# Chosen experts' inner activations turned by 32x32 blocks on VectorE and a trip through DRAM, instead of by TensorE

## The chip, the cores and the metric

The kernel runs on one core of one Trainium2 chip. The metric is the device time of one execution in microseconds (us), from the first to the last instruction of the core. Engine names in the profile: PE is TensorE's matmuls, PEld its weight loads, DVE is VectorE, ACT is ScalarE, POOL is GpSimd, SP is SyncE; a q behind a name (SPq) is that engine's sequencer, which issues DMAs.

## The reference, cut to what matters

Four layers with residuals follow each other. The change lies in the first, a mixture of experts over 64 batches of 64 tokens with 256 channels:

```python
rw = softmax(router_logits); w, sel = top_k(rw, 2)          # two experts of 8 for each batch
def _gemma_mlp(x, gate_w, up_w, down_w):                    # 256 -> 1024 -> 256
    g = einsum('bsh,hi->bsi', x, gate_w)
    u = einsum('bsh,hi->bsi', x, up_w)
    return einsum('bsi,ih->bsh', gelu(g) * u, down_w)       # gelu(g) * u: the inner activations
out = sum over the two chosen experts of w_e * mlp_e(x)  +  mlp_shared(x)
x = x + out            # then layers 1, 2 and 3, which the change does not touch
```

The product with `down_w` contracts over the 1024 inner channels, so for TensorE the inner activations must stand with channels, not tokens, on the partitions.

## The kernel before

Every engine has its own hand-written program; semaphores (`wait_ge`, `then_inc`) are the only order between them. Nothing is moved by a scheduler.

The batches are sorted by chosen expert. A group is 128 tokens: two batches with one expert (60 full groups), or two batches with two experts (four such pairs, each worked as two half groups; the code calls them mixed, `at.half` is 0 or 1). That makes NR0 = 68 group slots in a row, one loop of NMIXED0 = 4 rounds of BODY = 17 slots with two slots ahead of it and two behind. The groups before them belong to the shared expert, as do those after them, which are interleaved with layers 1 and 2. "Chosen stage" below is the stretch of these 68 slots, about 182 to 785 us of the span.

A full group has two halves (h = 0, 1) of 512 inner channels. For each, TensorE computes gate and up (`up_gate`, L713 to L715: three passes of float32r parts, 12 matmuls of 512 columns) with tokens on the partitions. ScalarE takes the gelu (L1242), VectorE multiplies with up into `hid` (L1744). TensorE then turns `hid` by four 128x128 transposes against `ident` into `turn_ps` in PSUM (`turn`, L783). ScalarE copies it as high part `hh` (`hidden_hi`, L1252), VectorE subtracts to get the low part `hl` (`hidden_lo`, L1751: one operand in PSUM, one in SBUF), and TensorE multiplies both with the down weights (`down`, L801 to L804). VectorE weighs and adds the result (`add`, L1815 and L1819), SyncE stores it to `chosen_rows` in DRAM (`store_chosen`, L355). In slot g TensorE's order is: up_gate half 0 of g, turn half 1 of g - 1, down half 0 of g - 1, up_gate half 1 of g, turn half 0 of g, down half 1 of g - 1. So down comes one slot behind up_gate.

VectorE also makes the low part of the next x (`split_x`, L1734: both operands in SBUF). GpSimd loads the float32 weights of the next expert in pieces of 512 KB into `raw` and splits each in two parts (`split`, L559 and L561: two operations on 1024 columns, SBUF to SBUF). It starts an expert's six pieces when the last group of the expert before last has been added, and then waits for the next such moment. There are eight such stretches of splitting in the chosen stage, about 34 us each. SyncE's queue holds, in program order per slot: the x loads for the slot after next (`load_skill`, waits for `xl_done`), in four of 17 slots two or four 512 KB pieces of weights for the mixed pair (`load_mixed0`, L363), and `store_chosen`, which waits for `acc_done`.

Of the kernel before, what the change touches and what calls it, by code (L numbers as in the profile page):

```python
# [31 lines left out]
F32 = mybir.dt.float32  # L32
F32R = mybir.dt.float32r
I32 = mybir.dt.int32
ALU = mybir.AluOpType
# [3 lines left out]
P = 128  # L39
NB, S, D = 64, 64, 256  # L40
E = 8
# [12 lines left out]
TURNLESS = 2 * (EARLY - FIRST)  # L54
# [41 lines left out]
FIRST_TWO = place_at(-1, BODY - 2), place_at(-1, BODY - 1)  # L96
LAST_TWO = place_at(NMIXED0, 0), place_at(NMIXED0, 1)


def build(nc, x, xT, cond, condT, w0, w1, mask, b1, w2, b2, w3, b3, out):  # L100
    mixes = nc.dram_tensor("mixes", (WPIECES, P, NU * P), F32, kind="Internal").ap()
    x3 = nc.dram_tensor("x3", (NB, S, D), F32, kind="Internal").ap()
    chosen_rows = nc.dram_tensor("chosen_rows", (NB, P, D), F32, kind="Internal").ap()

    with ExitStack() as ctx:
# [72 lines left out]
        hm = [acc[:, NSH + 25 + h, :] for h in range(2)]  # L178
# [66 lines left out]
        hh_done, hl_done = sem("hh_done"), sem("hl_done")  # L245
        down_done, acc_done, add_step = sem("down_done"), sem("acc_done"), sem("add_step")
# [33 lines left out]
        def table_values(engine, at, top):  # L280

            return nc.values_load_multi_w_load_instructions(
                at, engines=[engine.engine], min_val=0, max_val=top,
                skip_runtime_bounds_check_because="the routing bounds what the table holds")[1]

# [3 lines left out]
        def _(sp):  # L289
# [56 lines left out]
            def load_skill(g, p, at):  # L346
                slot = 2 * at.full if at.half is None else 2 * FULL0 + 2 * at.mixed
                batches = table_values(sp, source[0:1, bass.ds(slot, 2)], NB - 1)
                sp.wait_ge(xl_done, g - 1)
# [47 lines left out]
            for dst, src in ((b12, b1), (b2s, b2)):  # L397
                sp.dma_start(dst, src.rearrange("(a d) -> a d", a=1).broadcast_to([P, D])).then_inc(biases_in, 16)
            for c in range(DC):
                sp.dma_start(b1c[:, c:c + 1], b1[P * c:P * (c + 1)].rearrange("(p a) -> p a", a=1))\  # L400
                    .then_inc(biases_in, 16)
            for k in range(2):
                load_skill(S0 + 2 + k, k, place_at(0, k))
            for k in range(NSTAGE):
                sp.wait_ge(spilled[k], 16 * WPIECES // NSTAGE)
            with sp.Fori(0, NMIXED0) as m:
                for k in range(BODY):
                    g = S0 + BODY * m + k
                    load_skill(g + 4, k % 2, place_at(m, k + 2))
                    if k < 2:  # L410
                        load_mixed0(m, 0, ((0, 1, 2, 3), (4, 5))[k], S0 + BODY * m)
                    at = place_at(m, k - 2)
                    if at.half != 0:
                        store_chosen(g, k % 2, at)
                    if k in (HALVES[0] + 2, HALVES[0] + 3):
                        load_mixed0(m, 1, ((0, 1, 2, 3), (4, 5))[k - HALVES[0] - 2], S0 + BODY * m + HALVES[0] + 3)
# [12 lines left out]
            load_late(0)  # L429
            load_late(1)  # L430
            store_chosen(S1 - 4, 0, place_at(NMIXED0 - 1, BODY - 2))
            store_chosen(S1 - 3, 1, place_at(NMIXED0 - 1, BODY - 1))
# [255 lines left out]
        def _(pe):  # L688
# [49 lines left out]
            def up_gate_mixed(g, at, h):  # L738
# [3 lines left out]
                for ps, k, done in ((gate_ps[h], 0, gate_done), (up_ps[h], 1, up_done)):  # L742
                    if h == 0:
                        pe.wait_ge(mixed0_in[k], 64 * at.mixed + 32 * at.half + 32)
                    for c in range(DC):
                        part = slice(c * 512 + D * h, c * 512 + D * (h + 1))
                        mm = both_batches(ps, chunk(xm, c), [mixed0_w[2 * k + j][:, part] for j in range(2)], D,
                                          c == 0, c == DC - 1)
# [29 lines left out]
            def turn(h, n2, first=False, chunks=4):  # L778
# [3 lines left out]
                for c in range(chunks):  # L782
# [116 lines left out]
            def chosen_group(g, p, at, before_at):  # L899

                def before_down(h, e):
                    if before_at.half is None:
                        down(g - 1, 1 - p, h, e, 2 * g - 2 + h)
                    else:
                        down_mixed(g - 1, 1 - p, before_at, h)

                e = load_expert(at) if at.half is None else None
                for h in range(2):
# [4 lines left out]
                    if h == 0:  # L913
# [1233 lines left out]
```

## Time and profile before

| | us |
|---|---|
| median of 3 runs | 1191.1 |
| lowest and highest run | 1189.87, 1192.92 |
| span of the profiled execution | 1190.3 |
| median less that span | 0.8 |

The span is the profiled execution's own time: what lies around it is not recorded apart. A row of the profile names a line of the kernel, the engine and the operation, the tile written and the one read, and either one duration or the count, the sum and the mean. Matmuls are pipelined: their rows overlap, and the step from one start to the next is what one costs.

### The profile page before, as it was taken

To read this page: it belongs to the slowest core of one execution; us is meant where nothing else is said; L and a number is where in the kernel's file an instruction comes from. 1 tells how busy PE (TensorE), PEld (TensorE's weight loads), DVE (VectorE), ACT (ScalarE), POOL (GpSimd) and SP (SyncE) were. 2 spreads that over 40 slices of the span, in tenths; PEclk is the share of its full clock that TensorE was granted. 3 is DMA by queue.
4 is the path that set the end of the run, shared out by engine and by line. 5 is a ranking of instruction groups with operands and counts; after the bars stand their busy time and mean duration, and the time that the engine had idled before them with its cause. 6 is when DMAs were issued, how large, how long until landed. Compare 5 with 4: busy or idle time off the path is not lost.

```text
span 1190.3 us, 25584 instructions
## 1 busy us (share of the span) xinstructions
PE 1171.9 (98%) x7406; PEld 1001.3 (84%) x7407; DVE 613.2 (52%) x1119; ACT 435.0 (37%) x845; POOL 462.0 (39%) x296
## 2 busy tenths in 40 slices
PE   8999999999999999999999999999999999899998
PEld 7999998788787888878788787889999999678876
DVE  6775775444444444454544454456555555434443
ACT  4355532222222322222222222222222232566664
POOL 3277688108145045180635481010000000888840
PEclk9999999999999999999999999999999999999999
DMA  7279866243253324352253531046644446578653
GB/s 209 63 252 327 286 203 222 67 134 99 68 172 107 126 64 138 100 184 84 83 157 114 183 88 50 18 140 176 182 134 132 132 131 241 169 223 244 212 151 117
DMA packets 159578, 177.88 MB, mean 149 GB/s; under 512 B 68480, under 2 KB 134272, under 8 KB 157440
## 3 DMA queue, kind: packets, MB, share of 16 engines
q1 hardware_dynamic: 145808, 126.83, 35.1%
q0 software_dynamic: 13680, 49.81, 13.7%
q8 instruction: 61, 1.00, 0.3%
q14 instruction: 29, 0.24, 0.1%
HBM read 143.04 MB, written 33.55 MB: 148 GB/s over the span
## 4 chain that ended last, share of the span: by engine, by line
PE 91%; DMA 3%; DVE 2%; POOL 1%; SPq 1%; issue 1%; ACT 1%; ACTq 0%; POOLq 0%; DVEq 0%
PE bank L713 14%; PE bank L714 14%; PE bank L715 14%; PE bank L802 9%; PE bank L1152 6%; PE bank L783 5%; PE bank L734 4%; PE bank L801 4%; PE bank L1181 3%; PE bank L995 2%; PE bank L853 2%; PE bank L1130 2%; PE bank L855 2%; PE bank L854 2%; PE bank L1161 1%; PE bank L804 1%
## 5 line engine op out<-in xcount | busy, mean ns | idle before, releaser
L559 POOL TENSOR_TENSOR W<-raw,one 128x1024 fp32r<-128x1024 f32 x79 | 150.2, 1901 | 565.7 <-DVE acc L1815 269.5
L1744 DVE TENSOR_TENSOR FS<-bank,FS 128x512 f32<-128x512 f32 (+1 forms) x200 | 133.7, 669 | 320.5 <-PE bank L715 276.3
L1242 ACT ACTIVATE FS<-bank 128x512 f32<-128x512 f32 (+1 forms) x200 | 116.1, 580 | 326.4 <-PE bank L715 299.7
L713 PE MATMUL bank<-W,RS 128*128 (+1 forms) x512 | 202.8, 396 | 1.9 <-DVE W L1856 1.9
L714 PE MATMUL bank<-W,RS 128*128 (+1 forms) x512 | 200.6, 392 | 0.0
L715 PE MATMUL bank<-W,RS 128*128 (+1 forms) x512 | 200.3, 391 | 0.0
L561 POOL TENSOR_TENSOR W<-raw,W 128x1024 fp32r<-128x1024 f32 x79 | 191.8, 2428 | 6.2
L802 PE MATMUL bank<-W,RS 128*128 x480 | 188.6, 416 | 0.0
L1252 ACT ACTIVATE RS<-bank 128x512 fp32r<-128x512 f32 x128 | 76.6, 598 | 152.1 <-PE bank L783 152.1
L713 PE MATMUL bank<-RS,W 128*128 128x256 f32 x448 | 129.1, 288 | 1.0 <-DVE RS L1734 1.0
L715 PE MATMUL bank<-RS,W 128*128 128x256 f32 x448 | 126.6, 283 | 0.0
L714 PE MATMUL bank<-RS,W 128*128 128x256 f32 x448 | 126.6, 283 | 0.0
L713 PEld LDWEIGHTS bank<-W,RS 128*128 128x128 f32 x512 | 96.2, 188 | 25.7 <-issue 6.2
L715 PEld LDWEIGHTS bank<-W,RS 128*128 128x128 f32 x512 | 96.2, 188 | 21.1
L714 PEld LDWEIGHTS bank<-W,RS 128*128 128x128 f32 x512 | 96.2, 188 | 19.3
L1751 DVE TENSOR_TENSOR RS<-bank,RS 128x512 fp32r<-128x512 f32 x128 | 88.4, 691 | 35.7 <-ACT RS L1252 35.7
L801 PE MATMUL bank<-W,RS 128*128 x360 | 101.1, 281 | 0.0
L802 PEld LDWEIGHTS bank<-W,RS 128*128 128x128 f32 x480 | 90.6, 189 | 11.3
L713 PEld LDWEIGHTS bank<-RS,W 128*128 128x128 f32 x448 | 85.6, 191 | 1.3 <-issue 1.2
L783 PEld LDWEIGHTS bank<-ident,FS 128*128 128x128 f32 x544 | 67.2, 141 | 22.6 <-issue 6.2
L714 PEld LDWEIGHTS bank<-RS,W 128*128 128x128 f32 x448 | 85.7, 191 | 0.1
L715 PEld LDWEIGHTS bank<-RS,W 128*128 128x128 f32 x448 | 85.6, 191 | 0.0
(227 smaller groups left out, 2051.7 us busy)
## 6 DMA issues: line engine op xcount, KB each, us to landing
raw<-in_w POOLq DMA_DIRECT2D x87, 512.0 KB, 4.3
acc<-in_w SPq DMA_DIRECT2D x70, 512.0 KB, 4.7
mixes<-acc SPq DMA_DIRECT2D x16, 1024.0 KB, 6.3
W<-mixes SPq DMA_DIRECT2D x16, 1024.0 KB, 6.2
FS<-in_xT SPq DMA_DIRECT2D x200, 64.0 KB, 2.7
chosen_rows<-acc SPq DMA_DIRECT2D x64, 128.0 KB, 1.7
acc<-chosen_rows SPq DMA_DIRECT2D x128, 64.0 KB, 2.1
acc<-in_b SPq DMA_DIRECT2D x8, 640.0 KB, 10.9
```

The source lines that it names most:

```text
L559: pool.tensor_tensor(hi, raw[:, k, :], ones_like(PIECE), ALU.mult).then_inc(done, 1)
L561: pool.tensor_tensor(lo, raw[:, k, :], hi.bitcast(F32), ALU.subtract).then_inc(done, 1)
L713: pe.matmul(ps, ah, bh, start=(i == 0), stop=False)
L714: pe.matmul(ps, ah, bl, start=False, stop=False)
L715: mm = pe.matmul(ps, al, bh, start=False, stop=(i == n - 1))
L783: mm = pe.transpose(chunk(turn_ps[h], c), chunk(hid[h], c), ident[:, :])
L801: pe.matmul(ps, chunk(hl[h], c), w2_[:, 0, :], start=False, stop=False)
L802: mm = pe.matmul(both, chunk(hh[h], c), w2_, start=(h == 0 and c == 0), stop=(h == 1 and c == 3))
L1242: act.activation(gl[h][:, 0:n], gate_ps[h][:, 0:n], ACT.Gelu_apprx_tanh).then_inc(gelu_done, 1)
L1252: act.activation(hh[h], turn_ps[h][:, :], ACT.Copy).then_inc(hh_done, 1)
L1744: TT(hid[h][:, 0:n], up_ps[h][:, 0:n], gl[h][:, 0:n], ALU.mult).then_inc(hid_done, 1)
L1751: TT(hl[h], turn_ps[h][:, :], hh[h].bitcast(F32), ALU.subtract).then_inc(hl_done, 1)
```

## The change

TensorE no longer turns the chosen experts' activations. VectorE transposes each `hid` half in its 32x32 blocks (`hidden_squares`), SBUF to SBUF, into `square[h]`. ScalarE issues a DMA that writes this to a DRAM buffer `squares` (`write_square`, one per half, runs of 512 B), and SyncE issues one DMA per group that reads it back with the blocks in turned places into `hidT` in SBUF (`read_hidT`, 512 KB, runs of 1 KB). The copy to `hh` and the subtraction to `hl` now read `hidT` in SBUF, not PSUM. The down weights' rows are permuted on the host to fit the order in which the channels come out, and a mixed half takes every fourth block of gate and up columns. Down now comes two slots behind up_gate, and so do `add` and `store_chosen`. SyncE's bias loads and second late x load move behind the chosen stage.

The pieces below are in this order: SyncE (`read_hidT`, its loop), TensorE (`chosen_group`), ScalarE, VectorE.

```diff
+            def read_hidT(s, p, at):
+                n = D if at.half is None else P
+                if isinstance(s, int):
+                    sp.wait_ge(hl_done, 2 * (S0 + s))
+                sp.wait_ge(squares_out, 32 * s + 32)
+                sp.dma_start(hidT.rearrange("p (a y) -> p a y", a=4)[:, :, 0:n],
+                             squares[p].rearrange("(a i) (g y) -> (i g) a y", a=4, g=4)[:, :, 0:n])\
+                    .then_inc(hidT_in, 16)
...
+                for k in range(BODY):
+                    s, at = 2 + BODY * m + k, place_at(m, k - 2)
+                    if at.half != 0:
+                        load_skill(S0 + s + 2, k % 2, place_at(m, k + 2))
...
+                    if at.half != 0:
+                        store_chosen(S0 + s - 2, k % 2, at)
+                    else:
+                        load_skill(S0 + s + 2, k % 2, place_at(m, k + 2), added=S0 + s - 1)
+                    read_hidT(s, k % 2, place_at(m, k))
...
-                    if h == 0:
-                        turn(1, 2 * g - 1, chunks=4 if before_at.half is None else 2)
-                        before = load_expert(before_at) if before_at.half is None else None
-                    else:
-                        turn(0, 2 * g, chunks=4 if at.half is None else 2)
-                    before_down(h, before)
+                    if s == 0:
+                        down_shared(g - 2, 2 + h)
+                    elif s > 1:
+                        if h == 0:
+                            before = load_expert_at(s - 2)
+                        down_chosen(s - 2, h, before)
...
+            def write_square(s, p, h, at):
+                n = D if at.half is None else P
+                act.wait_ge(squared, 2 * s + h + 1)
+                act.dma_start(squares[p].rearrange("p (g y) -> p g y", g=4)[:, :, n // 2 * h:n // 2 * (h + 1)],
+                              square[h][:, 0:2 * n].rearrange("p (g x) -> p g x", g=4)).then_inc(squares_out, 16)
+            def hidden_hi_chosen(s, h, at):
+                act.wait_ge(hidT_in, 16 * s + 16)
+                act.wait_ge(down_done, 2 * (S0 + s) + h - 1)
+                if at.half is None:
+                    act.activation(by_chunk(hh[h]), turned_hid(h), ACT.Copy).then_inc(hh_done, 1)
...
+            def hidden_squares(s, h, at):
+                dve.wait_ge(hid_done, 2 * (S0 + s) + h + 1)
+                if not (isinstance(s, int) and s == 0):
+                    dve.wait_ge(squares_out, 32 * s)
+                dve.transpose(square[h][:, 0:n], hid[h][:, 0:n]).then_inc(squared, 1)
+            def hidden_lo_chosen(s, h, at):
+                dve.wait_ge(hh_done, 2 * (S0 + s) + h + 1)
+                if at.half is None:
+                    TT(by_chunk(hl[h]), turned_hid(h), by_chunk(hh[h].bitcast(F32)), ALU.subtract).then_inc(hl_done, 1)
```

The order in each engine's program, for a full group in the loop. On VectorE before, one slot with its two halves: hid is TENSOR_TENSOR FS<-bank,FS, the low part is RS<-bank,RS, the low part of x is RS<-FS,RS, or a COPY ahead of a mixed group.

```order
L1741 REGISTER_ALU [waits up_done,gelu_done]
L1744 TENSOR_TENSOR FS<-bank,FS 128x512 [waits turn_done]
L1751 TENSOR_TENSOR RS<-bank,RS 128x512 [waits hh_done]
L1730 REGISTER_ALU
L1732 COPY acc<-FS 128x128 [waits xh_done]
L1738 REGISTER_ALU
L1741 REGISTER_ALU [waits up_done,gelu_done]
L1744 TENSOR_TENSOR FS<-bank,FS 128x512 [waits turn_done]
L1751 TENSOR_TENSOR RS<-bank,RS 128x512 [waits hh_done]
L1815 ISA [waits acc_done,down_done]
L1815 TENSOR_SCALAR acc<-bank,weight 128x256
```

On VectorE now, the same stretch of a slot (X and acc are `square[0]` and `square[1]`, routing is `hidT`):

```order
L1819 TENSOR_TENSOR FS<-bank,FS 128x512 [waits squared]
L1826 REGISTER_ALU [waits hid_done]
L1827 STREAM_TRANSPOSE X<-FS 128x512 [waits squares_out]
L1788 REGISTER_ALU
L1792 TENSOR_TENSOR RS<-FS,RS 128x256 [waits xh_done]
L1813 REGISTER_ALU
L1819 TENSOR_TENSOR FS<-bank,FS 128x512 [waits squared,up_done,gelu_done]
L1827 STREAM_TRANSPOSE acc<-FS 128x512 [waits squares_out,hid_done]
L1832 TENSOR_TENSOR RS<-routing,RS 128x512 [waits hh_done] x2
L1896 ISA [waits acc_done,down_done]
L1896 TENSOR_SCALAR acc<-bank,weight 128x256
```

Each half has a transpose behind its product, and the two subtractions of the group before now stand together at the slot's end, ahead of the addition.

On ScalarE now, one slot (FS<-bank is the gelu, RS<-FS the high part of x, RS<-routing the copy to `hh` of the group before):

```order
L1276 ACTIVATE FS<-bank 128x512 [waits hid_done]
L1270 ACTIVATE RS<-FS 128x256 [waits up_done,xraw_in1]
L1288 ISA
L1289 DMA squares<-X 512x1x128 [waits squared]
L1273 REGISTER_ALU
L1276 ACTIVATE FS<-bank 128x512 [waits hid_done,gate_done]
L1294 ISA
L1297 ACTIVATE RS<-routing 128x512 [waits down_done,hidT_in]
L1288 REGISTER_ALU
L1289 DMA squares<-acc 512x1x128 [waits squared]
L1297 ACTIVATE RS<-routing 128x512 [waits down_done,hidT_in]
```

Before, each copy stood behind a gelu and waited for `turn_done`; now the two copies wait for the DRAM read, and the second write stands between them.

On SyncE now, one slot (before, the last two rows were not there):

```order
L369 REGISTER_ALU
L314 ISA [waits xl_done]
L314 DMA FS<-in_xT 128x2x64
L314 ISA
L314 DMA FS<-in_xT 128x2x64
L377 ISA [waits acc_done]
L377 DMA chosen_rows<-acc 128x256
L424 ISA
L425 DMA routing<-squares 128x4x256 [waits squares_out]
```

The read stands behind the store, and so behind the store's wait for the addition.

## Rows read from the trace of the kernel before

**Rows 1.** The page's busy times (us, share of the span, instructions).
```profile
PE 1171.9 (98%) x7406; PEld 1001.3 (84%) x7407; DVE 613.2 (52%) x1119; ACT 435.0 (37%) x845; POOL 462.0 (39%) x296
```
**Rows 2.** The chain that ended last, by engine, then by line.
```profile
PE 91%; DMA 3%; DVE 2%; POOL 1%; SPq 1%; issue 1%; ACT 1%; ACTq 0%; POOLq 0%; DVEq 0%
PE bank L713 14%; PE bank L714 14%; PE bank L715 14%; PE bank L802 9%; PE bank L1152 6%; PE bank L783 5%; PE bank L734 4%; PE bank L801 4%; PE bank L1181 3%; PE bank L995 2%; PE bank L853 2%; PE bank L1130 2%; PE bank L855 2%; PE bank L854 2%; PE bank L1161 1%; PE bank L804 1%
```
**Rows 3.** Timeline of TensorE, half a full group (start us, us, what).
```profile
200.39 0.60 PE L783 MATMUL bank<-ident,FS 128*128 128x128 f32 x4
200.74 0.48 PE L802 MATMUL bank<-W,RS 128*128 x1
201.06 0.28 PE L804 MATMUL bank<-W,RS 128*128 x1
...
202.24 0.39 PE L713 MATMUL bank<-W,RS 128*128 x1
...
204.97 0.60 PE L783 MATMUL bank<-ident,FS 128*128 128x128 f32 x4
```
**Rows 4.** Lines L1751 (whole span) and L1734 (225 to 780 us): min/median/max ns.
```profile
L1751 DVE TENSOR_TENSOR RS<-bank,RS x128: 678/691/693, 19.2 to 780.5; 128x512 fp32r<-128x512 f32 x128
...
L1734 DVE TENSOR_TENSOR RS<-FS,RS x56: 412/415/2385, 229.1 to 772.2; 128x256 fp32r<-128x256 f32 x56
```
**Rows 5.** Busy by stretch: PE, PEld, DVE, ACT, POOL, clock, DMA share, GB/s.
```profile
269.00:303.00 34.00, 34.00 (x194) 27.43 (x193) 17.31 (x28) 9.94 (x20) 28.82 (x17) 1.00 0.37 106
303.00:341.00 38.00, 38.00 (x201) 30.87 (x200) 16.05 (x31) 10.47 (x20) 0.60 (x1) 1.00 0.37 111
```
**Rows 6.** DMA issues of the whole span: count, KB each, median us to landing.
```profile
acc<-in_w SPq DMA_DIRECT2D x70, 512.0 KB, 4.7
...
W<-mixes SPq DMA_DIRECT2D x16, 1024.0 KB, 6.2
...
chosen_rows<-acc SPq DMA_DIRECT2D x64, 128.0 KB, 1.7
acc<-chosen_rows SPq DMA_DIRECT2D x128, 64.0 KB, 2.1
...
x<-raw SPq DMA_DIRECT2D x16, 256.0 KB, 2.2
```
**Rows 7.** Timeline behind a group's last down, and of SyncE's queue.
```profile
320.42 0.60 ACT L1252 ACTIVATE RS<-bank 128x512 fp32r<-128x512 f32 x1 [1.21 <-PE bank L783]
321.05 0.69 DVE L1751 TENSOR_TENSOR RS<-bank,RS 128x512 fp32r<-128x512 f32 x1 [0.22 <-ACT RS L1252]
321.93 0.48 DVE L1815 TENSOR_SCALAR acc<-bank,weight 128x256 f32<-128x256 f32 x1 [0.18 <-PE bank L802]
322.54 0.48 DVE L1819 SCALAR_TENSOR_TENSOR acc<-bank,weight,acc 128x256 f32<-128x256 f32 x1
323.19 0.35 SPq L355 DMA_DIRECT2D chosen_rows<-acc  x1
...
329.10 1.94 SPq L363 DMA_DIRECT2D acc<-in_w  x4
```
**Rows 8.** Timeline of GpSimd: first and second piece of an expert, next expert.
```profile
269.76 1.88 POOL L559 TENSOR_TENSOR W<-raw,one 128x1024 fp32r<-128x1024 f32 x1 [55.13 <-DVE acc L1815]
...
275.42 1.91 POOL L559 TENSOR_TENSOR W<-raw,one 128x1024 fp32r<-128x1024 f32 x1
...
341.01 1.88 POOL L559 TENSOR_TENSOR W<-raw,one 128x1024 fp32r<-128x1024 f32 x1 [37.37 <-DVE acc L1815]
```
**Rows 9.** L1734 alone, summed over six stretches in which GpSimd splits (us).
```profile
sum 203.00, DVE 26.58; mean DVE 4.43
```
**Rows 10.** The page's DMA queue of GpSimd: packets, MB, share of 16 engines.
```profile
q0 software_dynamic: 13680, 49.81, 13.7%
```
**Rows 11.** Timeline at the end of the chosen stage: turn of x1 waits.
```profile
791.30 0.65 PE L984 MATMUL bank<-ident,routing 128*128 128x128 f32 x4 [1.47 <-DVE routing L1919]
```

More of the change, by code:

```diff
@@ L53 @@
 NU = NSH // 2
-TURNLESS = 2 * (EARLY - FIRST)
 S0, S1 = EARLY, EARLY + NR0
@@ L177, in build @@
         xm, held, scaled = acc[:, NSH + 24, :], acc[:, NSH + 27, :], acc[:, NSH + 28, :]
-        hm = [acc[:, NSH + 25 + h, :] for h in range(2)]
+        hm = [acc[:, NSH + 31, :], routing[:, 5 * D:6 * D]]
+        square = [X1[:, :], acc[:, NSH + 25:NSH + 27, :].rearrange("p a d -> p (a d)")]
+        hidT = routing[:, 0:I0]
         chosen_out = [acc[:, NSH + 29 + r, :] for r in range(2)]
@@ L781, in turn @@
                     pe.wait_ge(hl_done, n2 - 1)
-                for c in range(chunks):
+                for c in range(4):
                     mm = pe.transpose(chunk(turn_ps[h], c), chunk(hid[h], c), ident[:, :])
@@ L897, in pair_shared, with down_chosen, load_expert_at, chosen_group @@
                     mix(2 * q + 1)
[L899 to L903, printed above, removed]
[L904 to L907 removed]
+            def down_chosen(s, h, e):
+                if place(s).half is None:
+                    down(S0 + s, s % 2, h, e, 2 * (S0 + s) + h)
+                else:
+                    down_mixed(S0 + s, s % 2, place(s), h)
+            def load_expert_at(s):
+                return load_expert(place(s)) if place(s).half is None else None
+            def chosen_group(s):
+                g, p, at, before = S0 + s, s % 2, place(s), None
+                e = load_expert_at(s)
                 for h in range(2):
@@ L1043, in _ @@
             pe.sem_inc(down3_done, 1)
-            last = load_expert(LAST_TWO[1])
             pe.wait_ge(split_step, 12 * SHARED_LATE + 12)
-            up_gate_late(0, 0, 0)
-            turn(1, 2 * S1 - 1)
-            down(S1 - 1, 1, 0, last, 2 * S1 - 2)
-            up_gate_late(0, 0, 1)
-            down(S1 - 1, 1, 1, last, 2 * S1 - 1)
+            for q in range(2):
+                up_gate_late(0, 0, q)
+                last = load_expert_at(NR0 - 2 + q)
+                for h in range(2):
+                    down_chosen(NR0 - 2 + q, h, last)
             up_gate_late(0, 0, 2)
@@ L1388, in _ @@
             gelu_late(0, 0)
-            hidden_hi(1, 2 * S1 - 1, skipped=TURNLESS)
+            for h in range(2):
+                hidden_hi_chosen(NR0 - 1, h, LAST_TWO[1])
             gelu_late(0, 1)
```

236 lines of the change are left out of this document (136 added, 100 removed).

## Prediction

> **What bounds the kernel now.** I read the page's busy times first: TensorE is busy 98% of the span, no other engine is above 52% [rows 1]. The chain that ended last says the same by another road: 91% of it is TensorE, and the transposes L783 have 5% of it by themselves [rows 2]. So time taken off TensorE counts fully, as long as nothing new makes it wait. Next I read the timeline of TensorE inside the chosen stage, for what a transpose really costs. Rows overlap there, so starts are what count: from one half's transposes to the next is 204.97 - 200.39 = 4.58 us [rows 3].
>
> **What is removed.** Four transposes push the next matmul's start back by 200.74 - 200.39 = 0.35 us, and the first down matmul behind them takes a step of 0.32 (to 201.06) where the 12 gate and up matmuls step by (204.97 - 202.24) / 12 = 0.23 [rows 3]. So 0.435 per half is gone: a half costs 4.14, a group 8.28 instead of 9.16. 60 full groups have 120 halves: 120 x 0.435 = 52.2. Each of 16 mixed halves turns two blocks, half of 0.35 and the same 0.09: 4.3. In all **-56.5**. The 32 transposes of the first four shared groups stay.
>
> **What is added.** Per group VectorE gets two transposes of 512 columns. No row shows one. The nearest operation with 512 columns takes 0.69 [rows 4]; I take 0.65, bounds 0.35 and 0.7. VectorE is busy 16.05 of 38 us while GpSimd rests [rows 5], 3.9 per group of 9.16, so 1.3 more fits into 8.28. The permuted weights cost nothing on the device: the matmuls keep their column counts and come behind each other as before.
>
> New is the way from `hid` to `hl`. It has one buffer, `hidT`, and this closes a loop across engines. By the order in front, SyncE reads group s + 1 only behind the store of group s - 1; that store waits for its addition; the addition stands on VectorE behind both subtractions of group s; the second of them needs ScalarE's second copy; that one stands behind the second write, and this behind the first copy, which waits for the read of group s. From one read's issue to the next:
> - the read lands. 64 KB take 2.1 and 1024 KB in runs of 512 B take 6.2 [rows 6]; on the line between, 512 KB take 4.0, and I take that, since size and runs lie between these two rows. Below: stores of 128 and 256 KB take 1.7 and 2.2, a line that gives 3.2. Above: 512 KB pieces take 4.7, say 5.0 with the writes and x loads beside it;
> - ScalarE starts (0.2) and copies (0.60) [rows 7];
> - it issues the second write: not shown for ScalarE; SyncE takes 0.35 for one and 1.94 / 4 = 0.49 in a row [rows 7]; I take 0.5;
> - the second copy 0.60, the subtraction 0.03 + 0.69, both additions 323.02 - 321.93 = 1.09 [rows 7];
> - SyncE sees it 0.17 later and issues the store in 0.35 [rows 7]; the read follows, say 0.14.
>
> Sum 4.0 + 0.8 + 0.5 + 0.6 + 0.72 + 1.09 + 0.66 = **8.37**, as good as the 8.28 that TensorE would like to take: +0.09 a group where nothing else works.
>
> Something else does. Each of eight stretches of splitting takes six pieces of 275.42 - 269.76 = 5.66 us, so 34 us, and GpSimd rests until the next [rows 8]; inside, it is busy 28.8 of 34 us [rows 5]. There an operation of VectorE with both inputs in SBUF is slow: L1734 is 0.415 in the middle of all [rows 4], but the 19 in six such stretches sum to 26.58 [rows 9], 1.40 each, 1.0 more. L1751, with one input in PSUM, never takes over 0.693 [rows 4]. The change moves this subtraction's input from PSUM to SBUF, so both subtractions join the slow kind. In the loop the second pays its 1.0, the first about 0.5 (the write and the second copy cover the rest). And the expert pieces share the DMA engines with the read: 13.7% of 1190.3 us [rows 10] over 95 pieces is 1.7 us of all 16 engines each, every 5.66 us, a share of 0.3, for which I add 0.4 to the read. The loop there is 8.37 + 1.5 + 0.4 = 10.3, **+2.0** over 8.28. 8 x 34 us hold 27 such groups: +54. The other 33: +3. In mixed groups the loop is shorter (half the bytes, short copies), but TensorE's work too; where only the downs are mixed it is 7.5 us against a loop of 8.37, beyond the 0.09 counted already: 8 x 0.7 = +5. Mixed weights come in eight sets of six 512 KB pieces, ahead of the read in SyncE's own queue and on the same engines; each set holds reads up by about 2 (between 1 and 3, one to two pieces' 1.7): +16. Slack takes off a little, once. Following the loop's terms from the last up matmul of a slot (6.9 into it), the read lands 7.6 into the next slot and `hl` is ready 0.9 into the one after, where it is needed at 2.73: -2. **Stalls +76.**
>
> At the end of the stage two groups' downs are left instead of one, and the rows that layer 1 needs are stored a slot later. There the turn of x1 already waits 1.47 [rows 11]; I add **+2** (0 to 6).
>
> A rule of the Trainium skill speaks against this change: SBUF — State Buffer, "Who interferes with whom", says that a VectorE instruction with two SBUF inputs and a GpSimd instruction that reads SBUF exclude each other wholly, while one with at most one SBUF input does not contend. By that rule, the trace agrees [rows 4, 9]. By the rule alone, with arrival at random in operations of 1.9 and 2.4 us every 5.66, the wait would be an estimated 0.8, not 1.0, and the time about 7 us lower.
>
> **The sum.** 1190.3 - 56.5 + 76 + 2 = 1211.8, against the profiled span; the median of the runs is 0.8 above that span: **1212** to 1213, slower by 1.8%.
>
> **The rivals.**
> - *All hidden (faster).* If the loop stays below 8.28 even while GpSimd splits, TensorE never waits: 1191.1 - 56.5 + 2 = 1137. For it speaks that down has a whole slot more than before; against it the 10.3. It needs a read that lands in 2.0.
> - *A short trip (faster).* With a read in 3.2 the loop is 7.6 outside a stretch and 9.5 inside. Inside it costs 27 x 1.2 = 32; between stretches each group wins back up to 0.7, so slack is there each time: 8 x 2.2 = -17; mixed weights +8; the end +2: 1191.1 - 56.5 + 25 = 1160. The forecast turns to this side where the read lands in about 3.7.
> - *Changes nothing.* Gain and stalls cancel at 57 of stalls: 1191. That is only a point between two cases.
> - *A crowded trip (slower still).* The read takes 5.0, since 1 MB of new traffic per group in short runs joins a DMA share of 0.37 [rows 5]. Loop 9.4 outside, 11.3 inside: 33 x 1.1 + 27 x 3.0 + 18 + 12 - 2 = 145: 1191.1 - 56.5 + 145 = 1279. On the way there, VectorE's transposes could wait for GpSimd too (one input in SBUF; no row shows it): 27 x 1.0 above the forecast, 1239.
>
> The Trainium skill (DMA: Bandwidth & Descriptors, "Anatomy of one DMA") gives a DMA a fixed 2.0 us and 436 GB/s; by it 512 KB would land in an estimated 3.2 us, the short trip's time. The 4.7 of [rows 6] for the same size does not agree with it.
>
> **How the numbers follow.** A measurement of this kernel tells about 0.3% (3.6 us) from no change. All hidden (up to 1148) has 0.10; a short trip (1148 to 1187) 0.24; within 0.3% 0.08; the forecast (1195 to 1240) 0.38; crowded (over 1240) 0.20. So faster 0.34, same 0.08, slower 0.58. The likeliest is 1212, its own range 1195 to 1240. From 1150 to 1265 leaves out about 0.11 below and 0.08 above.
>
> **What would show it.** In the timeline of TensorE a half of 4.14 us where it runs freely, and transposes only in the first four groups. TensorE idle in front of the first down half, released by VectorE's subtraction, most in the stretches where GpSimd splits and at mixed weights; about 75 us in all. The subtraction at 0.69 in quiet stretches, near 1.7 in the others. ScalarE waiting for the DMA into `hidT`, SyncE for the addition rather than for the writes. The read's median to landing near 4.0; a slot of 8.4 in quiet stretches, over 10 in the others. I am wrong if the read lands in 3.5 or less, if the subtractions do not slow down, or if SyncE's read waits for the writes (then they are the loop, not the addition).

## The result and the profile after

The changed kernel takes 1262.7 us (median of 4 runs, 1259.8 to 1270.6), against 1191.2 for the kernel before on the same chip: a ratio of 1.061, 95% interval 1.058 to 1.065. The forecast had the direction only: 1212 was meant as a loss of 1.8%, and the loss is 6.1%. The time lies outside the forecast's own range, 1195 to 1240, and just inside the wide one, 1150 to 1265; over 1240 the prediction had put its rival, the crowded trip, at 0.20. The profiled execution has a span of 1259.4 us. The medians and ratios below are of fast executions alone: one of the four of gelu_spread2, at 1251.5, was in the chip's slower state and is left out.

The page of the changed kernel: busy times, the chain that ended last (engines, then the head of the lines), and its DMA issues with KB each and median us to landing.

```profile
PE 1160.2 (92%) x6894; PEld 972.5 (77%) x6895; DVE 730.9 (58%) x1255; ACT 435.0 (35%) x845; POOL 466.7 (37%) x296
...
PE 46%; DMA 31%; DVE 9%; issue 5%; ACT 3%; SPq 3%; POOL 2%; ACTq 1%; DVEq 0%; POOLq 0%
...
acc<-in_w SPq DMA_DIRECT2D x70, 512.0 KB, 5.5
routing<-squares SPq DMA_DIRECT2D x60, 512.0 KB, 4.2
...
squares<-X ACTq DMA_DIRECT2D x60, 256.0 KB, 4.2
squares<-acc ACTq DMA_DIRECT2D x60, 256.0 KB, 3.1
FS<-in_xT SPq DMA_DIRECT2D x200, 64.0 KB, 3.5
```

`X` and `acc` are the places of `square[0]` and `square[1]`, `routing` that of `hidT`. Against [rows 1], TensorE has 512 matmuls fewer, yet is busy only 11.7 us less, and its idle time went from 18.4 to 99.2 us. DMA has 31% of the chain where it had 3% [rows 2].

Where TensorE runs freely, the gain is what was forecast. Its timeline over one half of a group (each row gives start, us, what; the step from the first row to the last is the half): 285.69 - 281.53 = 4.16 us instead of 4.58 [rows 3].

```profile
281.53 0.40 PE L752 MATMUL bank<-W,RS 128*128 x1
...
284.29 0.39 PE L842 MATMUL bank<-W,RS 128*128 x1
...
285.69 0.39 PE L752 MATMUL bank<-W,RS 128*128 x1
```

The waits of the chosen stage (182 to 860 us; total, times, longest):

```profile
ACT RS L1297 <- DMA routing<-squares: 131.7, 57, 5.8
...
DVE X L1827 <- DMA squares<-acc: 61.2, 20, 6.2
...
PE bank L842 <- DVE RS L1832: 48.9, 27, 5.4
...
PE bank L752 <- DVE RS L1792: 20.3, 10, 4.3
...
SPq L377 <- DVE acc L1903: 297.8, 62, 8.3
SPq L425 <- DMA squares<-acc: 60.4, 21, 6.1
```

ScalarE waits for the read (L1297), TensorE for the subtraction (L842 for L1832), SyncE's store for the addition: the loop of the forecast. (A row names the engine and line that waited, and what ended the wait.) Three rows speak of something else. VectorE's transpose (L1827) waits 61.2 us for a write of the slot before to land, since `square` can't be overwritten earlier; SyncE's read waits 60.4 us for a write; and TensorE waits 20.3 us at the first gate matmul, for the low part of x (L1792), which nothing in the forecast makes late.

**One slot with mixed weights.** The timelines of SyncE, ScalarE, VectorE and TensorE at 259 to 276 us, each in its own order of time:

```profile
259.75 0.49 SPq L425 DMA_DIRECT2D routing<-squares  x1
...
263.44 1.97 SPq L385 DMA_DIRECT2D acc<-in_w  x4
267.29 0.36 SPq L377 DMA_DIRECT2D chosen_rows<-acc  x1
272.99 0.39 SPq L425 DMA_DIRECT2D routing<-squares  x1
...
264.13 0.52 ACTq L1289 DMA_DIRECT2D squares<-acc  x1
...
272.99 0.71 DVE L1827 STREAM_TRANSPOSE X<-FS 128x512 f32<-128x512 f32 x1 [5.27 <-DMA squares<-acc]
273.63 0.38 DVE L1792 TENSOR_TENSOR RS<-FS,RS 128x256 fp32r<-128x256 f32 x1
...
274.42 0.79 PE L752 MATMUL bank<-W,RS 128*128 x1 [2.91 <-DVE RS L1792]
275.00 0.63 PE L753 MATMUL bank<-W,RS 128*128 x1
275.43 0.63 PE L754 MATMUL bank<-W,RS 128*128 x1
```

Four pieces of 512 KB are issued at 263.44; the write issued 0.7 us later lands only at 272.99, 8.9 us after its issue. Until then the read can't be issued, and VectorE stands at its transpose. Behind it in VectorE's queue is the low part of x, and so TensorE is idle 2.91 us with nothing wrong in the loads of x. From the read before to this one 13.2 us pass.

The same rows show the cost that the forecast left out altogether. Behind the idle time the matmuls step by 275.43 - 275.00 = 0.43 us instead of 0.23, until 280 us. The stretch 270 to 280 us of the view of windows (PE, PEld, DVE, ACT, POOL, then the granted clock, DMA share, GB/s):

```profile
270.00:280.00 10.00, 7.09 (x22) 5.50 (x21) 4.45 (x8) 2.65 (x5) 0.00 (x0) 0.69 0.71 212
```

The granted clock is 0.69 of full here, so TensorE ran at 1.2 GHz for a good part of the stretch and at 2.4 for the rest; over the whole span it was 1.000 before and is 0.967 now. The Trainium skill (TensorE: Matmul & The Clock Gate, "What's actually happening") states that an idle TensorE falls to 1.2 GHz and returns to 2.4 once it has been busy; by that rule, the trace agrees here.

Not every wait is followed by a lower clock. In the timeline of this stage (182 to 850 us) TensorE has 17 waits of 2.0 us or more. Behind 13 of them its matmuls step at half the rate at once or nearly so; behind the 3.91 us at 310.12 they do from the eighth matmul on; behind those of 2.28, 2.10 and 2.31 us (at 364.12, 765.50 and 776.43) they don't:

```profile
364.12 0.49 PE L752 MATMUL bank<-W,RS 128*128 x1 [2.28 <-DVE RS L1792]
364.45 0.40 PE L753 MATMUL bank<-W,RS 128*128 x1
```

**One stretch in which GpSimd splits.** VectorE's subtractions and SyncE's reads at 302 to 326 us:

```profile
309.01 3.48 DVE L1832 TENSOR_TENSOR RS<-routing,RS 128x512 fp32r<-128x512 f32 x2 [2.89 <-ACT RS L1297]
...
319.57 4.58 DVE L1832 TENSOR_TENSOR RS<-routing,RS 128x512 fp32r<-128x512 f32 x2 [3.13 <-ACT RS L1297]
...
302.57 0.38 SPq L425 DMA_DIRECT2D routing<-squares  x1
...
314.17 0.37 SPq L425 DMA_DIRECT2D routing<-squares  x1
...
325.83 0.37 SPq L425 DMA_DIRECT2D routing<-squares  x1
```

A pair of subtractions that takes 1.39 us in quiet (at 287.93) takes 3.48 and 4.58 here, and the reads step by 11.6 and 11.7 us. The two lines over the span (min/median/max ns):

```profile
L1832 DVE TENSOR_TENSOR RS<-routing,RS x120: 649/693/2909, 186.7 to 841.8; 128x512 fp32r<-128x512 f32 x120
...
L1827 DVE STREAM_TRANSPOSE X<-FS x68: 445/712/715, 174.1 to 828.1; 128x512 f32<-128x512 f32 x60, 128x256 f32<-128x256 f32 x8
```

So the subtraction joined the kind with two SBUF inputs [rows 4], as forecast; the transpose with one input never did.

**The loop where nothing else works.** SyncE and ScalarE at 227 to 236 us:

```profile
227.43 0.38 SPq L425 DMA_DIRECT2D routing<-squares  x1
235.13 0.37 SPq L425 DMA_DIRECT2D routing<-squares  x1
...
231.37 0.63 ACT L1297 ACTIVATE RS<-routing 128x512 fp32r<-128x512 f32 x1 [1.87 <-DMA routing<-squares]
231.45 0.52 ACTq L1289 DMA_DIRECT2D squares<-acc  x1
232.07 0.63 ACT L1297 ACTIVATE RS<-routing 128x512 fp32r<-128x512 f32 x1
```

From one read to the next 235.13 - 227.43 = 7.70 us pass, with the read, the copies, the addition and the store all in between. The forecast had 8.37. It put the issue of the second write between the two copies; in fact ScalarE's queue issues it beside the first copy, and the second copy starts 0.70 us behind the first.

### The profile page after: what moved, and what is told of

It is laid out like the page before. It is cut to its first block, busy times and chain, and to the rows that moved or that the text cites. A ratio compares the mean times of both kernels' runs of the same rounds, so it can differ in the third digit from the quotient of the medians.

```text
span 1259.4 us, 24975 instructions
## 1 busy us (share of the span) xinstructions
PE 1160.2 (92%) x6894; PEld 972.5 (77%) x6895; DVE 730.9 (58%) x1255; ACT 435.0 (35%) x845; POOL 466.7 (37%) x296
## 4 chain that ended last, share of the span: by engine, by line
PE 46%; DMA 31%; DVE 9%; issue 5%; ACT 3%; SPq 3%; POOL 2%; ACTq 1%; DVEq 0%; POOLq 0%
DMA routing<-squares 16%; DMA squares<-acc 12%; PE bank L752 6%; PE bank L753 6%; PE bank L754 6%; PE bank L1186 6%; DVE RS L1832 4%; PE bank L1215 3%; PE bank L1030 2%; ACT RS L1297 2%; PE bank L893 2%; PE bank L1164 2%; PE bank L895 2%; PE bank L894 2%; PE bank L842 1%
## 5 line engine op out<-in xcount | busy, mean ns | idle before, releaser
L842 PE MATMUL bank<-W,RS 128*128 x480 | 189.6, 417 | 49.4 <-DVE RS L1832 48.9
L752 PE MATMUL bank<-W,RS 128*128 (+1 forms) x512 | 212.3, 415 | 22.9 <-DVE RS L1792 20.6
L753 PE MATMUL bank<-W,RS 128*128 (+1 forms) x512 | 206.8, 404 | 0.0
L754 PE MATMUL bank<-W,RS 128*128 (+1 forms) x512 | 205.5, 401 | 0.0
L600 POOL TENSOR_TENSOR W<-raw,W 128x1024 fp32r<-128x1024 f32 x79 | 195.9, 2479 | 6.2
L1832 DVE TENSOR_TENSOR RS<-routing,RS 128x512 fp32r<-128x512 f32 x120 | 127.0, 1068 | 82.3 <-ACT RS L1297 81.8
L842 PEld LDWEIGHTS bank<-W,RS 128*128 128x128 f32 x480 | 93.2, 194 | 82.4 <-issue 67.8
L752 PEld LDWEIGHTS bank<-W,RS 128*128 128x128 f32 x512 | 101.2, 198 | 54.6 <-issue 33.6
L1819 DVE TENSOR_TENSOR FS<-bank,FS 128x512 f32<-128x512 f32 (+1 forms) x136 | 89.2, 656 | 86.7 <-ACT FS L1276 74.0
L752 PE MATMUL bank<-RS,W 128*128 128x256 f32 x448 | 131.0, 292 | 1.0 <-DVE RS L1792 1.0
L754 PE MATMUL bank<-RS,W 128*128 128x256 f32 x448 | 128.3, 286 | 0.0
L753 PE MATMUL bank<-RS,W 128*128 128x256 f32 x448 | 128.2, 286 | 0.0
L1297 ACT ACTIVATE RS<-routing 128x512 fp32r<-128x512 f32 x120 | 75.7, 631 | 148.1 <-DMA routing<-squares 131.7
L754 PEld LDWEIGHTS bank<-W,RS 128*128 128x128 f32 x512 | 100.1, 196 | 22.5
L753 PEld LDWEIGHTS bank<-W,RS 128*128 128x128 f32 x512 | 100.8, 197 | 20.5
L841 PE MATMUL bank<-W,RS 128*128 x360 | 103.6, 288 | 0.0
L752 PEld LDWEIGHTS bank<-RS,W 128*128 128x128 f32 x448 | 87.5, 195 | 1.3 <-issue 1.2
L753 PEld LDWEIGHTS bank<-RS,W 128*128 128x128 f32 x448 | 87.5, 195 | 0.1
L754 PEld LDWEIGHTS bank<-RS,W 128*128 128x128 f32 x448 | 87.3, 195 | 0.0
L1827 DVE STREAM_TRANSPOSE X<-FS 128x512 f32<-128x512 f32 (+1 forms) x68 | 46.3, 681 | 67.0 <-DMA squares<-acc 61.2
```

Source lines behind the costliest of these rows:

```text
L600: pool.tensor_tensor(lo, raw[:, k, :], hi.bitcast(F32), ALU.subtract).then_inc(done, 1)
L752: pe.matmul(ps, ah, bh, start=(i == 0), stop=False)
L753: pe.matmul(ps, ah, bl, start=False, stop=False)
L754: mm = pe.matmul(ps, al, bh, start=False, stop=(i == n - 1))
L841: pe.matmul(ps, chunk(hl[h], c), w2_[:, 0, :], start=False, stop=False)
L842: mm = pe.matmul(both, chunk(hh[h], c), w2_, start=(h == 0 and c == 0), stop=(h == 1 and c == 3))
```

## The experiments

All are edits of the changed kernel. The ratio is to the kernel before on the same chip; idle is the span less TensorE's busy time in the profiled execution. The span of a profiled execution can stand up to 10 us from the median of its kernel (1211.5 against 1221.3 for small_mixed), so the columns on the right are read in steps of that size. No_trip, lock_only, trip_only and those named `small_` leave out part of the work, as said at each.

| kernel | median us | ratio, 95% interval | PE busy | idle | clock |
|---|---|---|---|---|---|
| changed | 1262.7 | 1.061 (1.058 to 1.065) | 1160.2 | 99.2 | 0.967 |
| no_trip | 1146.7 | 0.963 (0.961 to 0.965) | 1119.8 | 27.2 | 0.994 |
| small_split | 1250.5 | 1.051 (1.048 to 1.054) | 1150.0 | 98.7 | 0.973 |
| small_loads | 1260.6 | 1.056 (1.051 to 1.060) | 1157.1 | 101.5 | 0.970 |
| small_mixed | 1221.3 | 1.026 (1.024 to 1.027) | 1136.0 | 75.5 | 0.983 |
| lock_only | 1211.3 | 1.016 (1.013 to 1.019) | 1144.2 | 70.1 | 0.976 |
| trip_only | 1163.9 | 0.977 (0.974 to 0.981) | 1125.6 | 36.0 | 0.993 |
| small_trip | 1206.0 | 1.013 (1.010 to 1.015) | 1137.8 | 62.7 | 0.986 |
| filler | 1305.8 | 1.099 (1.095 to 1.102) | 1268.5 | 30.1 | 0.996 |
| read_first | 1254.8 | 1.054 (1.051 to 1.056) | 1148.5 | 101.2 | 0.979 |
| write_first | 1257.8 | 1.055 (1.053 to 1.057) | 1149.9 | 110.4 | 0.981 |
| gelu_first | 1251.7 | 1.051 (1.047 to 1.055) | 1148.8 | 102.5 | 0.982 |
| spread | 1296.5 | 1.089 (1.084 to 1.093) | 1153.6 | 138.6 | 0.948 |
| gelu_spread | 1305.1 | 1.095 (1.092 to 1.099) | 1162.7 | 142.2 | 0.950 |
| spread2 | 1245.6 | 1.046 (1.043 to 1.050) | 1147.0 | 98.4 | 0.977 |
| gelu_spread2 | 1241.7 | 1.042 (1.033 to 1.050) | 1151.5 | 88.6 | 0.979 |

**No trip: what the removal alone is worth.** Write and read are left out from slot 2 on; VectorE still transposes, and `hh` and `hl` are made from what the first slots left in `hidT`.

```diff
 def read_hidT(s, p, at):
+    if not (isinstance(s, int) and s < 2): return
 def write_square(s, p, h, at):
+    if not (isinstance(s, int) and s < 2): return
 def hidden_hi_chosen(s, h, at):
-    act.wait_ge(hidT_in, 16 * s + 16)
+    act.wait_ge(hidT_in, 16 * s + 16 if isinstance(s, int) and s < 2 else 32)
 def hidden_squares(s, h, at):
-        dve.wait_ge(squares_out, 32 * s)
+        dve.wait_ge(squares_out, 32 if isinstance(s, int) and s == 1 else 64)
```

> Leaves out the trip through DRAM from slot 2 on: no write, no read and no wait for either; VectorE's transposes, the two subtractions from SBUF and the new order stay, and hidT keeps old data. Theory (the trip's loop and what it does to TensorE's clock cost about 125 us over the 1134.6 that the removed transposes alone would leave): 1135 to 1145, clock 0.99 or more, in spite of subtractions that GpSimd still slows. Rival (VectorE's added work and its waits for GpSimd are the bound by themselves): over 1180.

1146.7 us. TensorE's waits for the low part (total, times, longest):

```profile
PE bank L844 <- DVE RS L1836: 4.3, 3, 3.0
```

The slow subtractions are all there (mean 1101 ns), and cost next to nothing: without the loop VectorE's wait for GpSimd is hidden. The trip and what hangs on it are 1262.7 - 1146.7 = 116 us.

**Which load makes the trip dear.** GpSimd's splits, its loads of expert pieces, and the mixed weights are each cut from 1024 to 8 columns, GpSimd's from the third expert on. The other columns of those weights are left out; the trip is whole.

```diff
# small_split
-    pool.tensor_tensor(hi, raw[:, k, :], ones_like(PIECE), ALU.mult)
+    pool.tensor_tensor(hi, raw[:, k, 0:n], ones_like(n), ALU.mult)   # n = 8; the low part likewise
# small_loads
-    pool.dma_start(raw[:, k, :], src)
+    pool.dma_start(raw[:, k, 0:n], src)
# small_mixed
-    sp.dma_start(mixed0_w[k], w0[..., (3*half+i)*PIECE:(3*half+i+1)*PIECE] ...)
+    sp.dma_start(mixed0_w[k][:, 0:8], w0[..., (3*half+i)*PIECE:(3*half+i)*PIECE+8] ...)
# trip_only: all three.  lock_only: small_loads and small_mixed
```

> From the third expert on, GpSimd splits only 8 of 1024 columns of each piece (the rest of the weights stays old), so it no longer shares SBUF ports with VectorE for long; all DMAs stay. Theory (GpSimd's splits slow the two subtractions by 1.0 us and more each inside the loop): six of eight stretches no longer cost it, so 25 to 50 us less than 1263, that is 1213 to 1238, and every subtraction at 0.69. Rival (DMA traffic and latency alone hold the loop up): within 8 us of 1263.

> The mixed pairs' weight loads move 8 of 1024 columns of each of 48 pieces (the rest stays old), so 24 MB of 127 MB leave SyncE's queue. Theory (each set of them delays the trip by about 2 us and the delay halves TensorE's clock for a while): 20 to 35 us less than 1263. Rival (they are hidden, the slots after them are slow for other reasons): within 8 us of 1263.

> The changed kernel with GpSimd's loads of experts' weights cut to 8 of 1024 columns from the third expert on (the rest stays old), its splits at full length and pace, about 18 MB less traffic. With small_split it parts the two things that GpSimd does to the trip. Theory (the share of the DMA engines is the smaller part, 0.4 us of 1.9 a slot): 5 to 12 us less than 1263. Rival (traffic is the larger part, which small_split did not show because its loads came in one burst): 20 us or more less.

> small_split, small_loads and small_mixed together: from the third expert on GpSimd's loads and splits, and all mixed weight loads, are 8 columns long (weights stay old), so the trip through DRAM has the DMA engines and SBUF ports nearly to itself. Theory (nothing is wrong with the trip by itself, its step is at TensorE's 8.3 us; the cost is in what it meets): 1150 to 1175, near no_trip's 1147. Rival (the trip's own round is the bound, as a loop of 8.4 to 8.7 us would make it): 1185 or more.

> The changed kernel with the loads of the expert pieces and of the mixed weights cut to 8 columns from the third expert on, but GpSimd's splits at full width: its output is not the reference's. It stands between the kernel with all three cut (1164 us) and the one with only the mixed weights cut (1221). If the cost of the splitting stretches is the wait of the subtractions with two SBUF inputs for GpSimd, it stays near 1221: 1205 to 1220. If that cost is the traffic of the expert pieces on the DMA engines, it goes to 1164 to 1180.

With all three cut the kernel is at 1163.9, 2.3% faster than before: the trip itself, whose read still lands in 4.2 us, costs 17 us over no_trip. Put back one by one, in this order, the splits cost 47 (to 1211.3), the expert loads 10 (to 1221.3) and the mixed weights 41 (to 1262.7). The order matters: cut alone, the expert loads gave back 2 us (small_loads), which is inside the spread of the runs. VectorE's subtraction without and with the splits, in trip_only and in lock_only (busy, mean ns, idle before):

```profile
L1835 DVE TENSOR_TENSOR RS<-routing,RS 128x512 fp32r<-128x512 f32 x120 | 88.3, 738 | 69.4 <-ACT RS L1300 68.3
```

```profile
L1834 DVE TENSOR_TENSOR RS<-routing,RS 128x512 fp32r<-128x512 f32 x120 | 138.2, 1163 | 72.5 <-ACT RS L1299 71.8
```

and TensorE's wait for it, 9.9 us in trip_only, in lock_only:

```profile
PE bank L844 <- DVE RS L1834: 41.6, 20, 4.3
```

Small_split alone would have misled. With only the splits cut the kernel gained 12 us, not 47, although its subtractions are as short as in trip_only (749 ns). A split of 8 columns frees its buffer at once, so GpSimd issues the next load: three loads stand at 293.47, 295.31 and 297.05 us where the changed kernel issues one in 6 us, and the median landing of an expert piece went from 4.6 to 5.4. By this reading the cut took a cost away and made another; no run has the short splits with the old pace of the loads. Lock_only against trip_only has no expert or mixed traffic on either side and is the clean pair.

With the mixed weights cut, the new wait of VectorE is gone, 5.0 us where it had 61.2, and TensorE waits for x 3.2 instead of 20.3:

```profile
DVE X L1827 <- DMA squares<-acc: 5.0, 4, 1.6
...
PE bank L752 <- DVE RS L1792: 3.2, 3, 1.1
```

**A short trip.** Writes and reads move 16 columns in each run from slot 2 on, an eighth and a sixteenth of the bytes, so the order and all waits stay; the other columns are left out.

```diff
-    squares[p]...[:, :, n//2*h : n//2*(h+1)],  square[h]...
+    squares[p]...[:, :, n//2*h : n//2*h+16],   square[h]...[:, :, 0:16]
-    hidT...[:, :, 0:n],   squares[p]...[:, :, 0:n]
+    hidT...[:, :, 0:16],  squares[p]...[:, :, 0:16]
```

> The changed kernel with writes and reads of 16 columns in place of 128 and 256 from slot 2 on (data in hidT is mostly old): the same number of DMAs and descriptors, the same waits and order, an eighth and a sixteenth of the bytes. Theory (traffic is what stretches the trip: DMA busy 0.7 in the stage): a read then lands in 2.5 to 3.3 us, the loop is 7 us outside splitting, and the time is 1170 to 1205. Rival (latency and order alone hold the loop): within 15 us of 1263.

1206.0 us. The DMAs land in half the time (small_trip's list of DMA issues):

```profile
squares<-acc ACTq DMA_DIRECT2D x66, 32.0 KB, 2.1
routing<-squares SPq DMA_DIRECT2D x66, 32.0 KB, 2.1
```

and TensorE still waits 18.3 us for the low part and 17.6 for x. So the bytes of the trip, with what they do to the other transfers, are half of the 116 us (57), and what is left at a landing of 2.1 is still above the kernel before. The expected 1170 to 1205 was missed by 1 us.

**Is it the clock?** If TensorE's idle time costs more than itself, useless matmuls in its place should cost less than themselves.

```diff
+    if h == 0 and s > 2:
+        for _ in range(10):
+            pe.matmul(turn_ps[0][:, 0:P], ident[:, :], ident[:, :], start=True, stop=True)
```

> TensorE does ten extra 128-column float32 matmuls of ident into the idle bank ahead of the wait for the first down half in each slot, 0.9 us a slot, 57 us in all, and nothing else changes. Theory (an idle TensorE is granted the lower clock level afterwards, which costs about 40 us of the result): the extra work fills part of the idle time and saves part of the clock loss, so 1255 to 1275 and a mean clock of 0.98 or more. Rival (the clock follows the waits but costs nothing beyond them, and only the loop counts): the 57 us come on top where TensorE does not wait, 1285 or more, or with everything bound by the loop exactly 1263 at an unchanged clock of 0.97.

My estimate of the filler's own size was wrong. Its timeline:

```profile
306.75 2.39 PE L959 MATMUL bank<-ident 128*128 128x128 f32 x20
308.90 0.48 PE L842 MATMUL bank<-W,RS 128*128 x1
```

It is 308.90 - 306.75 = 2.15 us a slot, and with 1300 more records, 20 a slot, 65 x 2.15 = 140 us in all, an estimate from one slot. The time rose by 43 only. TensorE's idle time fell from 99.2 to 30.1 us, and its granted clock rose:

```profile
core 0: 1298.6 us, clock 0.996
```

and TensorE's wait for the low part, 48.9 us in the changed kernel, nearly went:

```profile
PE bank L842 <- DVE RS L1835: 4.1, 4, 1.7
```

Added work of 140 on a busy time of 1160.2 would be 1300; it is 1268.5, 32 us less. The DMAs and their bytes are the same as in the changed kernel and the clock is back, so it was the idle time that cost the clock, and not the traffic. The clock is a cost of its own: 69 (idle) + 32 (clock) is what the filler took back of its 140. As a test of 57 us it is void: the time fell into the range that was given to the rival, and the reading by busy time was made afterwards.

**The order around the read.** The read of group s + 1 is put ahead of the store of s - 1 (read_first), then also the second write ahead of the first copy (write_first), then also the second gelu ahead of the first write (gelu_first).

```diff
# read_first, SyncE
+    read_hidT(s, k % 2, place_at(m, k))        # waits hl_done
     store_chosen(S0 + s - 2, k % 2, at)
-    read_hidT(s, k % 2, place_at(m, k))
# write_first, ScalarE
+    write_square(s, p, 1, at)
     hidden_hi_chosen(s - 1, 0, before_at)
-    write_square(s, p, 1, at)
# gelu_first, ScalarE
+    gelu(1, 2 * g + 1, n=n)
     write_square(s, p, 0, at)
-    gelu(1, 2 * g + 1, n=n)
```

> All work is done. SyncE issues the read of a group ahead of the store, with a wait for the last subtraction (hidT free) in place of the store's wait for the addition, so additions and store (1.09 + 0.17 + 0.5 us) leave the loop. Theory (the loop read, copy, write, copy, subtraction, addition, store, read is the step where a slot is long): a slot in a splitting stretch goes from 11.5 to about 9.8, quiet ones stay with TensorE; 25 to 45 us less than 1263, that is 1218 to 1238. Rival (the writes' landing, or the weights in SyncE's queue, set the step): within 10 us of 1263.

> read_first, and ScalarE issues the second write ahead of the first copy, so a late read no longer delays the next group's second write. Theory (behind read_first the other loop, read, copy, second write, read, of about 4.2 + 0.8 + 3.1 + 0.3 = 8.4 us is next): 10 to 30 us less than read_first. Rival (only the loop through the subtractions counts): within 5 us of read_first.

> write_first, and ScalarE does the gelu of the second half ahead of the first write's wait for VectorE's transpose (ScalarE waited 170 us in all there). Theory (those waits are for the most part cover, ScalarE has time): 0 to 8 us less than write_first. Rival (this wait is in the step of the slow slots, since the second half's product and transpose stand behind it): 15 us or more less.

They gain 8, 5 and 11 us where 25 to 45 was expected of the first alone; the three hardly differ from each other beyond their intervals. The store and the additions leave the loop, and the write takes their place. SyncE's waits in read_first:

```profile
SPq L423 <- DVE RS L1831: 202.1, 54, 10.3
SPq L424 <- DMA squares<-acc: 109.5, 52, 6.3
```

For the changed kernel the write was in 21 of SyncE's waits, here in 52.

**Where the mixed weights are issued.** The pieces come behind the read, one piece a slot (spread); with gelu_first too (gelu_spread); the same with the first half's pieces two a slot (spread2, gelu_spread2).

```diff
-    if k < 2: load_mixed0(m, 0, ((0, 1, 2, 3), (4, 5))[k], ...)          # ahead of store and read
-    if k in (H + 3, H + 4): load_mixed0(m, 1, ((0, 1, 2, 3), (4, 5))[k - H - 3], ...)
     store_chosen(...); read_hidT(s, k % 2, place_at(m, k))
+    if k < 6: load_mixed0(m, 0, (k,), ...)      # spread2: if k < 3: load_mixed0(m, 0, (2*k, 2*k + 1), ...)
+    if H + 3 <= k < H + 9: load_mixed0(m, 1, (k - H - 3,), ...)
```

> All work is done. The mixed pairs' six pieces come one per slot, each behind the read, and not four and two ahead of it. Theory (small_mixed won 41 us because 2 MB at once stand ahead of the writes, the read and the next x): at least half of that comes back, 1222 to 1243. Rival (the bytes themselves cost the time, however they are placed): within 8 us of 1263.

> gelu_first with the mixed pieces spread as in spread. All work is done. Theory (the loops through additions, second write and gelu are cut there, so that with the pieces out of the way the quiet slots run at TensorE's pace, and only the splitting stretches, six pairs of slow subtractions each, stay): 1190 to 1225, less than spread by 10 to 30. Rival (the gains of both are the same time counted twice): within 5 us of spread.

> The changed kernel, with the twelve mixed weight pieces of a pass taken out of the place ahead of the read: those of the first half stand two by two behind the reads of slots 0, 1 and 2, those of the second half one by one behind the reads of slots 7 to 12. Theory A (what the mixed weights cost is their place ahead of a read and of the x loads): most of the 41 us that the loads of 8 columns gave comes back, 1225 to 1240 us. Theory B (the cost is their bytes on the DMA engines beside reads and writes, wherever they stand): within 8 us of the changed kernel, 1255 to 1270. Theory C (pieces behind the read are late for the up matmuls of the mixed groups, as with one piece a slot): 1275 or more, with TensorE waiting for the DMA into in_w.

> The same placement of the mixed weights together with the order in which the read stands ahead of the store on SyncE, and both writes and the second gelu ahead of the copies on ScalarE. If the two gains are apart from each other, the 11 us of that order come on top: 1215 to 1230 us. If both act on the same waits, it is no faster than the placement alone. In either case over 1191: neither touches the subtractions that GpSimd's splits hold up.

Spread was slower than the changed kernel by 34 us, and gelu_spread by 42, for a reason of my making: the pieces came after the mixed groups wanted them. TensorE's waits in spread, then in spread2:

```profile
PE bank L773 <- DMA acc<-in_w: 90.2, 13, 15.3
```

```profile
PE bank L842 <- DVE RS L1832: 54.9, 25, 4.4
PE bank L773 <- DMA acc<-in_w: 10.2, 4, 5.3
...
PE bank L752 <- DVE RS L1792: 3.7, 4, 1.3
```

Spread2 gains 17 of the 41 us, between the two theories: the wait for x is gone, so that one was placement, but TensorE's wait for the low part stays (54.9), and the first write's median landing is 5.6 instead of 4.2. The other 24 us went only when the bytes did; of these, pieces that are still somewhat late (10.2 us) are a part that was not taken apart. Both changes together (gelu_spread2) are no faster than the placement beyond the intervals. No version that does all the work came under the kernel before; the best is 4.2% over it.

## Why the prediction was right in direction and wrong in size

- **Removed, -56.5.** A half is 4.16 for 4.14. Without the trip TensorE's busy time is 52.1 us less, and idle 8.8 more, and the kernel gains 44.5. "All hidden, 1137" was out of reach by 10: even with the trip left out it is 1147.
- **Read landing 4.0.** 4.2 median (5.2 for two reads in the stretch of splitting at 300 to 326 us). The prediction's estimate of 3.2 by the Trainium skill (DMA: Bandwidth & Descriptors, "Anatomy of one DMA") is too low here; that section is on DMAs that GpSimd issues, and this read is SyncE's.
- **A quiet loop of 8.37.** Mis-sized: it goes round in 7.70, since the issue of the second write costs nothing. It didn't matter by itself, as TensorE takes 8.28 a group; in trip_only the reads step by 8.29 in the mean.
- **The transposes 0.65, not held up.** 0.71, longest 0.716. The rival in which GpSimd locks them out is refuted.
- **Splitting, 27 slots of 10.3, +54.** The mechanism was right, the pair is held up and only the loop makes it cost, but the number is right by luck. The +54 was meant as idle time. TensorE's idle time rises by 34.1 us from trip_only to lock_only and by 5.4 more with the expert loads (small_mixed), 39.5 in all; with the slower matmuls the time rises by 57. The slots aren't alike either: in lock_only 15 of the 67 steps from read to read are 11.0 us or more, about 3 longer than in trip_only, and most of the others are hardly touched.
- **Mixed weights, eight sets by 2, +16.** Their 41 us are again idle time and slower matmuls, about half each in the profiled executions (23.7 and 24.2, from small_mixed, whose span is 10 under its median), so as a stall the 16 was too low by some 4 to 8. The forecast let the pieces delay the read only; they delay the write ahead of it too (8.9 us instead of 3 to 4), and through VectorE's queue the x of the next group. "SyncE's read waits for the writes" stood among the signs of being wrong, and is what happens in those slots.
- **Stalls +76, end +2.** TensorE's idle time rose by 99.2 - 18.4 = 80.8. The total was right, in part by luck: 8.8 came without any trip where 2 was forecast, 8.8 with the trip alone (6 by the forecast's other terms), 39.5 with splitting and expert loads (54), 23.7 with mixed weights (16). The error of the time is elsewhere.
- **The sum, 1190.3 - 56.5 + 76 + 2: this step failed.** It priced a stall at its own length and left all else of TensorE at full clock. The same 6894 matmuls are busy 1119.8 us at a clock of 0.994 and 1160.2 at 0.967: 40.4 us, which the forecast had at nothing without a reason. Of these, 37.5 lie in the chosen stage (598.0 at a clock of 0.95 against 560.4 at 0.99). The difference of the clocks alone, 0.033 x 1259 less 0.006 x 1147, gives 35. The account is then 1190.3 - 52.1 + 40.4 + 80.8 = 1259.4, which closes by the way it is made up (busy and idle time), and so is no further proof; the filler is. With the missing term the forecast would have been some 1250. The rule of the Trainium skill that was cited above stood ready and wasn't weighed; rows of before could not show it, since its TensorE never waits over 2.6 us and its clock is 1.000.
- **Crowded trip, 1279.** The time lies in the range of this rival (over 1240) and nearer to it than to the forecast, but its mechanism, a read of 5.0 everywhere, isn't the one found: the median is 4.2.

What stays open: why some waits of 2.1 to 2.3 us cost the clock and others don't, since no run placed them one by one; how the 24 us of the mixed weights' bytes divide; and why gelu_first, with the shortest loop of the three orders, keeps slots of 11.6 us in splitting. No run took VectorE's lock away while all the traffic stayed evenly spread.

## What to carry to other kernels

Work taken off a TensorE that is busy 98% of the time pays only while what replaces it never lets TensorE stop: a stall is paid once as idle time and again, here with half as much on top, in slower matmuls behind it. When a loop across engines comes as near to the engine that it feeds as this one (7.7 and 8.28 us, before anything disturbs it), look at what stands in its queues and what runs beside it, not at its sum: operations whose slowness was hidden before (the subtraction held up by GpSimd) turn into the bound. And a wait for a DMA stops everything behind it in that engine's queue, as the transpose at 272.99 us did, so follow the queue of the engine that waits, as well as the data.

## What the runs showed of the hardware

- Behind an idle time of 2.91 us TensorE's matmuls stepped by 0.43 us, from 0.23, for over 5 us; behind 2.20 us, at 321.79, too, for 3 us; behind 2.28 us, at 364.12, and 2.31 us, at 776.43, they didn't, nor behind 0.47 us, at 289.04. So the length of the wait alone doesn't tell.
- With the idle time filled by useless matmuls, and the same DMAs (filler), the granted clock rose from 0.967 to 0.996.
- VectorE's 32x32 transpose of 128x512 float32 takes 0.71 us (0.45 for 256 columns), SBUF to SBUF; of 136 none took over 0.716, beside GpSimd's splits too.
- Two subtractions in a row with both inputs in SBUF can take 3.5 to 4.6 us beside GpSimd's splits of 1.9 and 2.5, against 1.39.
- A write of 256 KB in runs of 512 B lands in 3.1 and 4.2 us (the medians of the two halves), and in 8.9 with 2 MB of loads issued just ahead of it on another engine's queue.
